# Layer-norm columns, first loads and input statistics of a chunked decoder kernel, rearranged over VectorE, ScalarE and GpSimd

## The reference, cut to what matters

```python
def _L0_attn_ref(x, ln_g, ln_b, w_qkvb, b_qkvb, w_out, b_out):
    mu = jnp.mean(x, axis=-1, keepdims=True)
    var = jnp.mean((x - mu) ** 2, axis=-1, keepdims=True)
    normed = (x - mu) * lax.rsqrt(var + LN_EPS) * ln_g + ln_b
    proj = normed @ w_qkvb + b_qkvb
    q, k, v, beta_pre = jnp.split(proj, 4, axis=-1)
    beta = jax.nn.sigmoid(beta_pre)
    ...
    k = k / jnp.maximum(jnp.linalg.norm(k, axis=-1, keepdims=True), NORM_EPS)
    def step(S, inp):
        q_t, k_t, v_t, beta_t = inp
        retrieval = jnp.einsum('bhij,bhj->bhi', S, k_t)
        S = S + jnp.einsum('bhi,bhj->bhij', beta_t * (v_t - retrieval), k_t)
        o_t = jnp.einsum('bhij,bhj->bhi', S, q_t)
        return (S, o_t)
    _, out_t = lax.scan(step, S0, (q, k, v, beta))
    return x + scan_out @ w_out + b_out

x = x + _L0_attn_ref(_layernorm(x, axis=-1), ...)
```

## Time and profile before

| | us |
|---|---|
| median of three runs | 1123.03 |
| the profiled execution | 1123.51 |
| its span, first to last instruction | 1121.8 |
| PE busy | 933.7 (83%) |
| DVE busy | 926.6 (83%) |
| ACT busy | 663.2 (59%) |
| POOL busy | 434.6 (39%) |

### The profile page before, as it was taken

How to read it: one execution, slowest core, us unless ns; L and a number is a source line. 1 busy time by engine, 2 the same in 40 slices (tenths; PEclk the granted TensorE clock), 3 DMA queues, 4 the chain that set the end, 5 groups by cost and what they waited for, 6 DMA issues and landing times.

```text
span 1121.8 us, 19571 instructions
## 1 busy us (share of the span) xinstructions
PE 933.7 (83%) x6107; PEld 709.0 (63%) x6114; DVE 926.6 (83%) x2750; ACT 663.2 (59%) x1603; POOL 434.6 (39%) x655
## 2 busy tenths in 40 slices
PE   7688999999999999999999989899797610696056
PEld 7466777877887878878788777666565410343044
DVE  4767699999999999999999997666665879799887
ACT  2467566766566666666666653546575532586097
POOL 4323345465364553644535443315366660000000
PEclk8789799999999999999999998899988955798589
DMA  9900000000300000000000000213200000000012
GB/s 139 139 1 6 5 7 10 6 9 9 117 11 6 7 10 6 10 7 6 11 6 9 8 5 11 84 58 127 99 1 0 1 0 0 1 1 1 0 62 89
DMA packets 30150, 30.49 MB, mean 27 GB/s; under 512 B 7137, under 2 KB 25441, under 8 KB 30049
## 3 DMA queue, kind: packets, MB, share of 16 engines
q1 hardware_dynamic: 28128, 29.12, 10.8%
q10 hardware_dynamic: 1920, 0.14, 0.2%
HBM read 20.85 MB, written 4.19 MB: 22 GB/s over the span
## 4 chain that ended last, share of the span: by engine, by line
PE 64%; DVE 23%; ACT 6%; issue 5%; DMA 1%; ACTq 1%; DVEq 0%
PE ps L1770 7%; PE ps L1778 7%; PE ps L1709 5%; PE psG L1732 5%; DVE work L1645 5%; PE psY L1746 4%; PE psX L1746 4%; PE ps L1890 4%; PE psY L1824 3%; PE psY L1911 3%; PE psX L1824 3%; PE psG L1726 3%; PE ps L1838 2%; PE psX L1911 2%; PE psG L1890 2%
## 5 line engine op out<-in xcount | busy, mean ns | idle before, releaser
L510 POOL TENSOR_TENSOR arena<-arena 128x256 f32<-128x256 f32 x32 | 23.3, 729 | 306.5 <-DVE arena L1078 303.3
L603 ACT ACTIVATE arena<-ps 128x512 f32<-128x512 f32 x128 | 72.9, 596 | 48.1 <-PE ps L1770 47.9
L1770 PE MATMUL ps<-work 32*128 32x256 f32 x512 | 93.5, 406 | 2.4 <-ACT work L649 2.3
L478 POOL TENSOR_SCALAR_AFFINE_SELECT arena<-arena 128x2048 f32<-128x2048 f32 x32 | 92.1, 2879 | 2.2
L568 ACT ACTIVATE arena<-ps,nparity 32x256 f32<-32x256 f32 x124 | 51.1, 458 | 49.4 <-PE ps L1709 49.0
L1732 PE MATMUL psG<-arena 128*128 128x512 f32 x128 | 73.6, 658 | 2.4 <-DVE arena L1144 2.4
L1770 PEld LDWEIGHTS ps<-work 32*128 32x128 f32 x512 | 61.9, 186 | 19.4 <-issue 12.9
L1709 PE MATMUL ps<-work,arena 128*128 128x64 f32 x496 | 63.8, 285 | 6.7 <-DVE work L1104 6.7
L1089 DVE TENSOR_TENSOR arena<-arena 128x256 f32<-128x256 f32 (+1 forms) x96 | 66.5, 692 | 3.3
L1092 DVE TENSOR_REDUCE arena<-arena 128x64 f32<-128x256 f32 (+1 forms) x96 | 65.9, 687 | 3.3
L1746 PEld LDWEIGHTS psY<-work,arena 128*128 128x128 f32 x512 | 60.4, 196 | 12.4 <-DVE arena L1161 10.7
(11 more groups left out here) (328 smaller groups left out, 2612.0 us busy)
## 6 DMA issues: line engine op xcount, KB each, us to landing
arena<-in_mask_BxSxS_ik SPq DMA_DIRECT2D x8, 1024.0 KB, 6.7
xs<-arena SPq DMA_DIRECT2D x256, 16.0 KB, 1.8
arena<-in_ctx SPq DMA_DIRECT2D x8, 512.0 KB, 4.1
out<-xs SPq DMA_DIRECT2D x32, 128.0 KB, 1.7
arena<-in_x SPq DMA_DIRECT2D x8, 384.0 KB, 24.0
arena<-in_L_ffn_w SPq DMA_DIRECT2D x2, 1024.0 KB, 24.2
arena<-in_L_attn_w_qkvb SPq DMA_DIRECT2D x2, 512.0 KB, 5.8
arena<-in_x SPq DMA_DIRECT2D x8, 96.0 KB, 7.7
```

Source lines behind the costliest of these rows:

```text
L478: G.affine_select(out=pairs, in_=pairs, compare_op=ALU.is_ge, fill=0.0, base=0, pattern=[[0, NH], [-CT, B], [0, CT]], channel_multiplier=1 ...
L603: A.activation(attn[j % 2][:, r * 512:(r + 1) * 512], ps[(2, 0)[r % 2]][:, :], ACT.Copy).then_inc(att_out, 1)
L1770: last = M.matmul(ps[(2, 0)[r % 2]][:, f * 2 * P:(f + 1) * 2 * P], kq[j % 4][rows, f * P:(f + 1) * P], qe[rows, f].rearrange("p e t -> p ( ...
```

## The change

- **Loads.** The first group is chunks 0 to 3, the second 4 to 7. ScalarE's queue takes three of the first group's eight loads, SyncE's five. ScalarE's queue first issues three loads of `ln_g`, `ln_b` and `b_qkvb` as 12 rows of 128; TensorE turns them after 16 warm-up matmuls, VectorE copies them into `columns`, and 24 more warm-up matmuls follow.
- **VectorE's start.** `floors` is set, the columns are copied, the parities are made (they stood after the statistics), then statistics and factors of chunks 0 to 3. Group 1 (chunks 4 to 7) follows, its Newton steps and factors spread among the work for chunk 0. Where these write and read scratch, it is in PSUM (`root_of`), and with `floors` and `ones` as second tensors.
- **Root of chunk 0.** `first_root` on VectorE takes the place of GpSimd's `key_norms(0)`.
- **Late statistics.** `input_moments` on ScalarE is gone. VectorE has `bn_stats` of chunks 8 to 31 in slots 0, 3, 5, 7, 8, 9 (4, 6, 2, 4, 4, 4 of them), `input_variances` in slots 1, 4, 10, and three Newton steps with `input_factors` in slots 2, 6, 11, all between `keys_turned` and `state(j + 1)`; the single block in slot 2 is gone.
- **Seeds.** The shift and the subtraction of the inverse root's seed become one instruction, everywhere.
- **TensorE.** `far_gram(0)`, `near_gram(0)` stand earlier among the projections of chunk 2; in slot 0 `far_gram(1)` and `norms_turned(2)` follow all four attention parts.

```diff
-X_GROUPS = [(0, 2), (2, 8), (8, NCK)]
+X_GROUPS = [(0, 4), (4, 8), (8, NCK)]
+WARM = 24
+STAT_GROUPS = [(0, 4), (4, 8), (8, 12), (12, 18), (18, NCK)]
+STATS_AT = {0: (8, 12), 3: (12, 18), 5: (18, 20), 7: (20, 24), 8: (24, 28), 9: (28, NCK)}
+MOMENTS_AT = {1: 2, 4: 3, 10: 4}
+FACTORS_AT = {2: 2, 6: 3, 11: 4}
...
-            for b in range(B // 2):
+            for b in range(5):
                 load_x(sp, 0, b)
...
-            for m in range(3):
+            for m in (1, 2):
                 key_norms(m)
...
-                if j < 3:
-                    input_moments(j)
-                elif j < 5:
+                if 3 <= j < 5:
...
+            for k, vec in enumerate((ln_g, ln_b, b_qkvb)):
+                act.dma_start(vector_rows[DC * k:DC * k + vec.shape[0] // P, :],
+                              vec.rearrange("(c p) -> c p", p=P)).then_inc(vec_in, 16)
+            for b in range(5, B):
                 load_x(act, 0, b)
...
-                own(V.tensor_scalar(dst.bitcast(I32), t.bitcast(I32), 1, None, ALU.logical_shift_right))
-                own(V.tensor_scalar(dst.bitcast(I32), dst.bitcast(I32), -1.0, SEED, ALU.mult, ALU.add))
+                own(V.tensor_scalar(dst.bitcast(I32), t.bitcast(I32), -0.5, SEED, ALU.mult, ALU.add))
+
+            def newton_step(dst, t, m):
+                own(V.tensor_tensor(m, dst, dst, ALU.mult))
+                own(V.scalar_tensor_tensor(m, m, -0.5, t, ALU.mult, ALU.mult))
+                own(V.scalar_tensor_tensor(dst, m, 1.5, dst, ALU.add, ALU.mult))
...
+            def input_variances(k):
...
+                own.issue(V.tensor_tensor(total, a, b, ALU.add))
+                apart_known = own.issue(V.tensor_tensor(apart, a, b, ALU.subtract))
+                own.issue(V.tensor_tensor(squares, c, e, ALU.add))
+                own.need(apart_known)
+                own(V.tensor_tensor(apart, apart, apart, ALU.mult))
+                own(V.scalar_tensor_tensor(squares, apart, 0.25 * D, squares, ALU.mult, ALU.add))
...
+            def root_of(k):
+                n0, n1 = STAT_GROUPS[k]
+                if k < 2:
+                    return psY[:, 16 * k:16 * k + 2 * (n1 - n0)].rearrange("p (e n) -> p e n", e=2)
+                return variances[:, :, n0:n1]
...
-            for k in range(2):
-                v.wait_ge(x_in[k], 16 * B)
-                input_stats(*X_GROUPS[k])
-            v.wait_ge(consts, CONSTS)
+            for e, floor in enumerate((LN_EPS, LN_EPS * LN_EPS)):
+                own(V.memset(floors[:, e, :], floor))
+            v.wait_ge(vec_T, 1)
+            V.tensor_copy(columns[:, :], ps[2][:, 0:6 * DC]).then_inc(vec_ready, 1)
+            v.wait_ge(vec_ready, 1)
+            v.wait_ge(consts, 3)
...
             own(V.tensor_scalar(nparity[:, :], parity[:, :], -1.0, None, ALU.mult))
...
+            v.wait_ge(x_in[0], 16 * B)
+            input_stats(0, 4)
+            input_variances(0)
+            for _ in range(3):
+                input_step(0)
+            input_factors(0)
...
             key_norms(0)
+            first_root()
...
+                if j in STATS_AT:
...
+                    input_stats(*STATS_AT[j])
+                if j in MOMENTS_AT:
+                    input_variances(MOMENTS_AT[j])
+                if j in FACTORS_AT:
+                    for _ in range(3):
+                        input_step(FACTORS_AT[j])
+                    input_factors(FACTORS_AT[j])
                 if exists(j + 1):
                     state(j + 1)
```

More of the change, by code:

```diff
@@ L1015, in rsqrt @@
                 for _ in range(3):
[L1016 to L1032 removed]
+                    newton_step(dst, t, m)
             def input_stats(n0, n1):
@@ L1037, in input_stats @@
                     own.issue(V.bn_stats(stats[:, n, :], xc[:, n, :]))
+            def input_variances(k):
+                n0, n1 = STAT_GROUPS[k]
+                a, b, c, e = (stats[:, n0:n1, i] for i in (1, 4, 2, 5))
+                total, apart, squares = (T[i][:, n0:n1] for i in range(3))
+                t = root_of(k)
                 own.need(own.k)
-                a, b, c, e = (stats[:, n0:n1, k] for k in (1, 4, 2, 5))
-                total, apart, squares = (T[k][:, n0:n1] for k in range(3))
                 own.issue(V.tensor_tensor(total, a, b, ALU.add))
@@ L1046, in input_stats, with input_step, input_factors @@
                 own(V.scalar_tensor_tensor(squares, apart, 0.25 * D, squares, ALU.mult, ALU.add))
-                input_factors(n0, n1, total, -0.5, squares)
+                for e, (by, floor) in enumerate(((1.0, LN_EPS), (1.0 + LN_EPS, LN_EPS * LN_EPS))):
+                    if k == 0:
+                        own.issue(V.scalar_tensor_tensor(t[:, e, :], squares, by / D, floors[:, e, :], ALU.mult, ALU.add))
+                    else:
+                        own.issue(V.tensor_scalar(t[:, e, :], squares, by / D, floor, ALU.mult, ALU.add))
+                own.need(own.k)
+                seed(factors[:, :, n0:n1], t)
+            def root_of(k):
+                n0, n1 = STAT_GROUPS[k]
+                if k < 2:
+                    return psY[:, 16 * k:16 * k + 2 * (n1 - n0)].rearrange("p (e n) -> p e n", e=2)
+                return variances[:, :, n0:n1]
+            def input_step(k):
+                n0, n1 = STAT_GROUPS[k]
+                newton_step(factors[:, :, n0:n1], root_of(k), newton[:, :, n0:n1])
+            def input_factors(k):
+                n0, n1 = STAT_GROUPS[k]
+                total, mu, sh, rs, both = (t[:, n0:n1] for t in (T[0], mean, shift1, rstd, scale1))
+                own.issue(V.scalar_tensor_tensor(sh, total, -0.5, rs, ALU.mult, ALU.mult))
+                own(V.scalar_tensor_tensor(rs, rs, 1.0, ones[:, 0:n1 - n0], ALU.mult, ALU.add))
+                V.scalar_tensor_tensor(mu, total, -0.5, both, ALU.mult, ALU.mult).then_inc(stat_ready, 1)
+                own.need(own.k)
             def ternary_factors():
@@ L1170, in key_norms, with first_root @@
                 ss, root, _ = nrm
-                squares, half = ps[1][:, 0:NH], ps[1][:, NH:2 * NH]
+                squares = ps[1][:, 0:NH]
                 own(V.tensor_scalar(squares, squares, -1.0, NORM_EPS * NORM_EPS, ALU.mult, ALU.max))
                 own.issue(V.tensor_copy(ss, squares))
-                own(V.tensor_scalar(half.bitcast(I32), squares.bitcast(I32), 1, None, ALU.logical_shift_right))
-                own(V.tensor_scalar(root.bitcast(I32), half.bitcast(I32), -1.0, SEED, ALU.mult, ALU.add))
+                own(V.tensor_scalar(root.bitcast(I32), squares.bitcast(I32), -0.5, SEED, ALU.mult, ALU.add))
                 v.sem_inc(seeded, 1)
+            def first_root():
+                ss, root, sqr = nrm
+                for n in range(3):
+                    own(V.tensor_tensor(sqr, root, root, ALU.mult))
+                    own(V.scalar_tensor_tensor(sqr, sqr, -0.5, ss, ALU.mult, ALU.mult))
+                    if n < 2:
+                        own(V.scalar_tensor_tensor(root, sqr, 1.5, root, ALU.add, ALU.mult))
+                wide = [t.rearrange("p (h a) -> p h a", a=1).broadcast_to([P, NH, HD]) for t in (sqr, root)]
+                V.scalar_tensor_tensor(rn_wide.rearrange("p (h d) -> p h d", d=HD), wide[0], 1.5, wide[1],
+                                       ALU.add, ALU.mult).then_inc(rn_ready, 1)
             def keys_turned(m):
@@ L1918, in _ @@
             pe.wait_ge(consts, 1)
-            for _ in range(42):
-                M.matmul(psY[:, 0:P], ones[:, :], ones[:, :], start=True, stop=True)
+            for _ in range(16):
+                M.matmul(psX[:, 0:P], ones[:, :], ones[:, :], start=True, stop=True)
             pe.wait_ge(consts, 4)
+            pe.wait_ge(vec_in, 48)
+            M.transpose(ps[2][:, 0:6 * DC], vector_rows, ident[0:6 * DC, 0:6 * DC]).then_inc(vec_T, 1)
+            for _ in range(WARM):
+                M.matmul(psX[:, 0:P], ones[:, :], ones[:, :], start=True, stop=True)
             turn(0)
```

84 lines of the change are left out of this document (30 added, 54 removed).

## The result

| | before | changed |
|---|---|---|
| median of 8 runs, us | 1121.55 | 1130.97 |
| lowest to highest, us | 1111.60 to 1125.03 | 1127.16 to 1134.75 |
| the profiled execution, us | 1123.51 | 1127.16 |
| its span, us | 1121.8 | 1125.4 |
| `start_chunk(1)`, us | 76.01 | 67.45 |

The ratio is 1.011, with an interval of 1.008 to 1.015: a small but measurable loss, under 2%. The forecast was 1131, within 2% of before. The starts are those of the profiled executions, one of each kernel. The changed kernel's is the fastest of its eight, so the spans differ by 3.6 us where the medians differ by 9.4.

The account below looks back on a forecast made before the run. The prediction took TensorE and VectorE as both near their limit in the recurrence. Start, fill with slot 0, slots 1 to 11, clock, seeds: 1123.5 - 11.3 + 12.4 + 7 - 1 = 1131 us; range 1104 to 1147.

Parts of the forecast that it names:

- The hold: Slots 1, 2, 4, 6, 10, 11: VectorE's late statistics wait for GpSimd's selects; slots 1 to 11 together +12.4 us.
- The clock: TensorE at half clock after stalls in slots 1, 2, 4, 6, 10, 11: 1.2 us each, +7 us.
- rival B: Each of the six TensorE stalls followed by 11.7 us at 1.2 GHz: 27 us instead of 7, 1151 us; chance 0.12.
- The fill: Up to start_chunk(0): 4.5 us earlier, at 35.1; with slot 0, start_chunk(1) at 64.7, -11.3 us in all.
- rival C: Fill gives little: late loads or half clock before 21 us make start_chunk(1) 4 to 6 us later, 1136 us; chance 0.12.
- The seeds' saving and the later stages: Later stages: 0.2 us saved at each of some 12 inverse roots, part of it hidden; -1 us.
- A: Late statistics not held by the selects, or only partly: slots 1 to 11 -6.8 us, 1104 to 1105 us; chance 0.18.

Follow-up runs that it names:

- TensorE kept busy: Changed kernel with 10 or 14 dummy TensorE matmuls ahead of the retrieval in slots 1, 2, 4, 6, 10, 11; 1116.89 us, ratio 0.998.
- the longer warm-up: Changed kernel with 34 instead of 24 warm-up matmuls on TensorE ahead of its first turn; 1127.21 us, ratio 1.007.
- the hold removed: Changed kernel with late variances, Newton steps and factors moved to just ahead of start_chunk, behind GpSimd's selects; 1107.85 us, ratio 0.989.

## Why the prediction was right, step by step

**The hold: right in mechanism, off by one or two instructions.** L1017 and the first L996 were to be held; L1020, L997 and (slot 11) L996 were. A few short instructions still start before the second select does. All the same each hold ends with the select, and that end, not the number of instructions held, sets the slot. TensorE's stalls were 2.45 to 4.45 us, where 4 to 5 had been forecast. The instructions behind it were priced too high: 0.65 us for 1.2 after L1020 (83.98 to 84.62), 1.58 for 2.1 after L997 (108.07 to 109.65). With TensorE kept busy, slots 1 to 11 take 248.7 where the forecast had 253.0 without the clock; this over-pricing, some 0.55 us in six slots, is 3.3 of the 4.3 (the kept-busy kernel still has 3.4 us of half clock, so the true figure is a little more).

**The clock: 9.7 us, not 7.** The difference between the changed kernel and the one kept busy is 258.35 - 248.67. The 1.2 us for each of six stalls should have been 1.6. The stretches of half clock, 3.4 and 6.8 us, stayed under the 7 us that would have meant rival B. The two errors are of opposite sign: 253 + 7 = 260 against 258.35 measured. The sum was nearer than its terms.

**The fill: 8.6 us, not 11.3.** `nparity` ended at 9.29 and ScalarE normalised at 14.28, as forecast (9.3, 14.3). The step that failed was "its projections ... take 2.9 for three": TensorE stood 2.46 us between warm-up and turn and ran them at 1.2 GHz, 5.33 us. That is rival C's mechanism, at half its price, and the longer warm-up shows it: the forecast starts came out to 0.1 us once the gap was closed. As nine kernels show gaps of 1.07 to 2.46 us there, the hit to 0.1 us is in part chance. Slot 0 took 29.64 us for 29.6 forecast: `state` started 22.2 us into it (22.6 forecast), and the retrieval at half clock behind it took 6.02 us and held the next `start_chunk` by 1.08.

**The seeds' saving and the later stages** were put at -1. The steady slot stays 20.21 us, and VectorE's wait at `state` grew instead, from 0.33 in the earlier trace rows to 0.56 once the last late block is past:

```profile
502.16 1.38 DVE L1162 TENSOR_TENSOR arena<-ps,arena 32x512 f32<-32x512 f32 x2 [0.56 <-PE ps L1745]
```

So there the saved instruction is hidden by TensorE, as the earlier trace rows would have it. From chunk 12 to the end of the span the profiled execution of before takes 805.2 us, the changed kernel's 799.6 and the other ten kernels', which all have the new seeds, 797.1 to 802.5. Of the 5.6 us, 5.3 lie behind `start_chunk(31)` (419.5 against 414.2 us), more than the 1 forecast. The medians, less the same starts, do not bear this out: 805.0 for before, 805.2 for the changed kernel, 798.6 to 807.7 over all twelve. With one profiled execution of each, how much the later stages gained, and whether by the seeds, stays open.

**The sum.** At chunk 12 the forecast had 12.4 + 7 - 11.3 = 8.1 us of loss, and 9.24 were measured: the fill gave 2.7 us less, the slots cost 1.6 us less. The sum started from 1123.5 us, and before's median is 1121.55; so the forecast change is 7.5 us and the measured one 9.4. That 1130.97 met 1131 so closely is chance; that there is a loss of some 9 us is not.

**The rivals.** A (no hold) is excluded by 2.80 us at L1020. Its price was also wrong: with the hold removed slots 1 to 11 take 241.55, not 233.8, so the time was 1108 and not 1104 to 1105; 13.6 us of half clock in slots 3 and 7 are in that. B (11.7 us at half clock behind each stall) did not come: the stretches were 3.4 and 6.8 us, the retrieval behind each stall lost 1.7 to 3.2 us (5.41 to 6.99 for 3.76), and the price of the six was 9.7, where B had 27. But one stretch of B's kind did come later, the 13.7 us behind slot 10's stall in the kernel with the longer warm-up. C is answered above, under the fill.
